# Row scatters of the first feed-forward block: the memset behind each one is left out

## The reference

```python
x = x + 0.5 * ffn(layernorm(x))
x = x + attn(layernorm(x))          # 16 heads of 8, causal, 2 x 1024 tokens
x = x + 0.5 * ffn(layernorm(x))

def ffn(x):                         # one shared and 7 routed experts, hidden width 352, top 2
    expert = lambda h, g, u, d: (silu(h @ g.T) * (h @ u.T)) @ d.T
    probs = softmax(x @ wr.T + rb)
    scores, idx = top_k(probs, 2);  scores = scores / scores.sum(-1)
    w = sum(scores * one_hot(idx))
    return expert(x, sg, su, sd) + sum(w[e] * expert(x, rg[e], ru[e], rd[e]) for e in range(7))
```

## Time and profile before

| what | value |
|---|---|
| median of 3 runs | 571.84 us (570.95 to 572.29) |
| profiled execution, own time | 571.84 us |
| its span, first to last instruction | 570.0 us |
| PE / PEld busy | 521.1 us (91%) / 406.0 us (71%) |
| DVE / ACT busy | 388.5 us (68%) / 319.8 us (56%) |
| POOL busy | 272.1 us (48%) |
| mean granted PE clock | 0.972 |
| indirect DMAs of the sort in f = 0 (L1174) | 32, 34.4 us busy, 24.8 to 77.1 us |
| memsets at L1184 into the scratch tensor | 66 in both blocks, 0.43 us each |

### The profile page before, as it was taken

The page is one execution under the profiler, slowest core; times in us unless marked ns, Lnnn a source line. Parts: engine busy times, 40 slices in busy tenths (PEclk is TensorE's granted clock), DMA queues, the critical chain, the costliest instruction groups (busy, mean ns, idle before and its releaser), DMA issues.

```text
span 570.0 us, 11374 instructions
## 1 busy us (share of the span) xinstructions
PE 521.1 (91%) x3574; PEld 406.0 (71%) x3574; DVE 388.5 (68%) x1013; ACT 319.8 (56%) x678; POOL 272.1 (48%) x417
## 2 busy tenths in 40 slices
PE   5985969999996799999999999999999889889995
PEld 2884969998954465656666666565746889889995
DVE  5694635557367888887979888888555775445744
ACT  4552424457444276776767677677776444434643
POOL 8299887667356711212120303030318888854540
PEclk9899789999996899999999999999999999999999
DMA  8922424132861581505050505020001031431414
GB/s 283 294 67 50 111 77 120 45 107 81 242 183 56 170 190 35 173 2 175 2 174 1 176 0 176 1 102 2 2 2 33 31 91 43 118 92 34 125 50 121
DMA packets 41384, 54.65 MB, mean 96 GB/s; under 512 B 6064, under 2 KB 32176, under 8 KB 40560
## 3 DMA queue, kind: packets, MB, share of 16 engines
q1 hardware_dynamic: 32528, 42.70, 26.4%
q0 software_dynamic: 4480, 9.25, 4.9%
q10 hardware_dynamic: 4320, 1.98, 1.3%
HBM read 34.03 MB, written 28.00 MB: 109 GB/s over the span
## 4 chain that ended last, share of the span: by engine, by line
PE 57%; issue 18%; POOL 10%; DMA 6%; DVE 4%; SPq 2%; ACT 2%; ACTq 1%; another core or an unknown queue 1%; POOLq 0%; DVEq 0%
PE psum L1605 11%; PE psum L1648 11%; PE psum L1677 10%; PE psum L933 6%; POOL z_rows L1174 6%; PE psum L919 3%; PE psum L901 3%; PE psum L899 3%; PE psum L900 3%; PE psum L1608 2%; POOL idle L1184 2%; DMA b_p<-in_attn_c_proj_b 2%; DMA yc<-y_rows 1%; DMA y_rows<-ys,to_row 1%; PE psum L1633 1%
## 5 line engine op out<-in xcount | busy, mean ns | idle before, releaser
L1757 DVE TENSOR_REDUCE mxp<-psum 128x1 f32<-128x512 f32 (+3 forms) x304 | 179.0, 654 | 32.9 <-PE psum L1605 32.1
L1816 ACT ACTIVATE probs<-psum 128x512 f32<-128x512 f32 (+1 forms) x304 | 154.9, 578 | 39.8 <-PE psum L1648 37.2
L1863 POOL TENSOR_SCALAR_AFFINE_SELECT probs<-probs 128x512 f32<-128x512 f32 x64 | 40.0, 635 | 174.2 <-ACT probs L1816 174.2
L1648 PE MATMUL psum<-queries,keys 128*128 128x512 f32 (+3 forms) x384 | 122.5, 381 | 0.6 <-DMA queries<-m_rows 0.3
L1605 PE MATMUL psum<-keys,queries 128*128 128x512 f32 (+1 forms) x304 | 116.1, 417 | 2.9 <-DVE mxp L1757 2.4
L1000 ACT ACTIVATE silu<-psum 128x352 f32<-128x352 f32 x107 | 49.6, 463 | 99.5 <-PE psum L901 62.6
L1197 POOL DMA_INDIRECT y_rows<-ys,to_row x76 | 74.3, 977 | 59.1 <-DVE ys L1079 35.4
L1043 DVE TENSOR_TENSOR act<-silu,psum 128x352 f32<-128x352 f32 x107 | 55.6, 519 | 68.0 <-ACT silu L1000 41.7
L933 PE MATMUL psum<-wall_f,at 128*128 (+1 forms) x648 | 92.2, 279 | 2.7 <-DVE x L1081 1.8
L1648 PEld LDWEIGHTS psum<-queries,keys 128*128 128x128 f32 x384 | 66.8, 191 | 26.8 <-ACT probs L1816 12.6
L933 PEld LDWEIGHTS psum<-wall_f,at 128*128 128x128 f32 x648 | 82.1, 194 | 4.1 <-ACT at L1008 2.3
(11 more groups left out here) (240 smaller groups left out, 732.4 us busy)
## 6 DMA issues: line engine op xcount, KB each, us to landing
z_rows<-q_stack SPq DMA_DIRECT2D x12, 682.5 KB, 5.6
keys<-k_stack SPq DMA_DIRECT2D x32, 128.0 KB, 5.9
queries<-q_stack SPq DMA_DIRECT2D x8, 512.0 KB, 5.3
zg_early<-z_rows SPq DMA_DIRECT2D x44, 65.0 KB
yc<-y_rows SPq DMA_DIRECT2D x10, 256.0 KB, 4.0
zg_late<-z_rows SPq DMA_DIRECT2D x32, 65.0 KB
k_stack<-zt_h SPq DMA_DIRECT2D x8, 256.0 KB, 2.9
q_stack<-q_h SPq DMA_DIRECT2D x8, 256.0 KB, 3.7
```

The costliest lines, as they stand in the source:

```text
L1648: ins = e.matmul(slot(K, u, d, n)[:, m * (q1 - q0):(m + 1) * (q1 - q0)], K.keys[v][:, j, kt * P:(kt + 1) * P], K.queries[v][:, q0:q1], sta ...
L1757: e.tensor_reduce(K.mxp[:, heads[0]:heads[-1] + 1, i, which], scores, AX.X, ALU.max).then_inc(K.A["taken"], 1)
L1816: e.activation(probs_of(K, product)[:, heads[0]:heads[-1] + 1, :], src, ACT.Exp, scale=SCALE).then_inc(K.A["ex"], 1)
```

## The change

In sort_pool the memset behind the indirect DMA is now written only for f = 1. In f = 0 the 30 memsets behind the DMAs of tiles 1 to 7 (14, part 0) and 8 to 15 (16, part 1) are gone. The indirect DMAs, their order, their data and their semaphores are the same, as are the memsets of f = 1 and those behind the first ten scatters of y_rows in both blocks.

```diff
     e.indirect_dma_start(K.z_dram[f], bass.IndirectOffsetOnAxis(ap=K.slots[:, g:g + 1], axis=0),
                          K.zrow[f][:, t, :], None).then_inc(K.z_sc[t // HALF], 16)
-    if g % TT > 0:
+    if f == 1 and g % TT > 0:
         pause_pool(K, f == 1 and t < HALF)
```

## The result

The changed kernel takes 578.38 us (median of 4 runs, 577.09 to 579.91) and the kernel before, on the same chip, 571.76 us (4 runs, 570.95 to 572.29). The medians differ by 6.6 us. The ratio is worked out from all 35 recorded runs of the changed kernel (575.98 to 582.40 us, mean 579.37): 1.0134, with a 95% interval of 1.0101 to 1.0168. It is slower. Two executions of the kernel before on the chips of the later experiments were in a slower state (578.63 and 730.11 us), and the ratios leave them out. The prediction was 560.8 us, with a range that ended at 566.8. It was wrong in sign. The profiled execution after took 579.51 us with a span of 577.7 (571.84 and 570.0 before); its granted clock was 0.968 (0.972).

A forecast was written before the change was run, and what follows sets the result against it. PE bounds the kernel, with two waits set by the end of POOL's scatters. 8.65 us gained at step 21 plus 2.4 us of clock, 11.05 in all, take 571.84 to 560.8 us; range 558.6 to 566.8.

The forecast's parts named there:

- Pitch: POOL's scatters in f = 0: start to start 1.26 us instead of 1.56, 0.30 us gained per removed memset.
- rival C: Scatter pitch stays 1.56 us without memsets, limited by DMA engines or POOL's descriptor making; time 571.8 us; chance 0.07.
- The 16th: Last scatter of the first half of the f = 0 sort: to end at 48.3 us instead of 52.10, 3.8 us earlier.
- DVE: Small DVE instructions held by denser scatters: each 0.55 us better or worse at most, 2.7 us on PE's path; nothing taken.
- The first wait of PE: PE before the first sorted transposes: there at 51.53, starts at 52.6 instead of 56.44, wait 1.1 us instead of 4.9.
- a sign of being wrong: PE's first sorted tiles (step 13): the prediction is wrong if PE comes to them later than 52.5 us.
- 1.2 us to spare: Places for the 17th scatter: written until 47.39, ahead of its possible start at 48.6, so not the later wait.
- The clock: PE's granted clock held through shortened waits: 2.65 us less after the first wait, 2.4 us more behind the second.
- Part 1: Second 16 scatters of f = 0: 4.8 us shorter, 32nd ends at 68.5; step 21 at 73.4 instead of 82.05.
- The time behind it: From 88 us on: PE at 9 tenths, everything behind released by it, so the gain stays; f = 1 shifted, not shortened.
- Rival D: DVE, needing the memset gaps, held until 48.3 and 18 us late, PE's shared tiles with it; 580 us; chance 0.06.

The follow-up runs named there:

- part 0 alone: Kernel before with only the 14 memsets of the first 16 scatters in f = 0 left out, the other 16 kept: 572.81 us, ratio 0.9993.

## Why the prediction was wrong

**Pitch (right).** It was 1.26 us in all of f = 0 without DVE's long subtractions, so rival C (1.56 stays) falls. The 16th ended 2.4 us earlier than forecast. The first scatter began 1.4 us earlier in that execution (23.37 instead of 24.77), and only three scatters met a long subtraction instead of four: DVE, late itself by then, started the fourth at 48.22 instead of 43.40, behind the 16th scatter. The working had kept DVE's subtractions in their places.

**DVE (right, as far as it went).** No instruction of DVE waited for the end of a run of scatters: L784 takes 0.17 us and L1482 1.25 in the middle of one. DVE's timeline of the changed kernel:
```profile
27.16 1.25 DVE L1482 TENSOR_TENSOR wall<-nat_g,wall 128x1056 fp32r<-128x1056 f32 x1
28.53 0.17 DVE L784 TENSOR_SCALAR d_cnt<-d_cnt 128x8 f32<-128x8 f32 x1
...
51.66 0.17 DVE L750 CAST slots<-d_slot 128x16 int32<-128x16 f32 x1
```
The rule of the Trainium skill (SBUF — State Buffer, "Who interferes with whom") was weighed as the one that speaks against the change. By it, an instruction of DVE loses at most one scatter; the largest lateness here is several scatters long and is measured on ACT as well as on DVE, so it isn't that rule at work.

**The first wait of PE (the step that failed).** The prediction said "PE is there at 51.53, since the tiles of the shared expert don't depend on the scatters". By data they don't. But each of their steps goes from PE to ACT to DVE and back, and with the scatters at 1.26 us each hand-over from PE came up to 5.0 us late. PE was there at 56.03 instead of 51.53, and it began the sorted tiles at 55.88, past the 52.5 that the prediction named as a sign of being wrong. With it the places of part 1 came at 51.84, 4.45 us late. The 1.2 us to spare that the prediction had worked out for them went with the rest, and the 17th scatter started at 52.65 instead of 48.6.

**The clock (followed from it).** The forecast held it at full speed, because waits were to be short. PE waited 7.38 and 5.15 us instead, and the mean from 53 to 73 us was 0.74 (0.83 before). It also fell ahead of the first wait: from 45.79 to 49.20 us it was at the lower level of 1.2 GHz, where it was at full speed before.

**Part 1 (its first half right).** 32nd scatter forecast for 68.5, seen at 72.54, all of which is the late start; its 16 pitches are 1.26 us. But step 21, forecast at 73.4, came at 91.01. It no longer waits for the sort at all: PE's down product L933 is right ahead of it, without an idle gap. PE was late by its own steps, held up to 8.2 us each in part 1, and the list rows_at came at 86.82 instead of 73.02 for the same reason.

**The time behind it (right).** Whatever step 21 is early or late by stays in good part to the end: it was late by 8.96 us and the span is 7.7 longer; the last scatter of y_rows in f = 0 starts at 165.58 instead of 158.96, 6.6 us late, which is also the difference of the medians.

**Rival D (right number, wrong cause).** It gave 580 us, slower, "the memsets are what lets DVE in", and PE's shared tiles late with DVE. The loss has this form and nearly this size, but what the gap lets in is PE's increments, and it had a chance of 0.06. The argument that lowered it (L853 and L750 end with the scatter they meet) was about one engine. There was no row in the profile before that showed a run of scatters at 1.26 us with PE's hand-overs beside it, only two scatters in a row. The gap was priced at what it costs, 0.30 us, and not at what it may be there for; its range below nothing was left out.

**What stays open.** Which resource fills is not shown: all that the traces show is that increments of PE and issues of SP are late together while POOL issues indirect DMAs densely. PE's ends are modelled by the profile, so it isn't shown either whether PE's last write or its increment is what waits. Every execution on record was also recorded for its spans, so whether the recording itself is a part of the load is untested. Nor is it shown how much of the difference between the parts is more than their pitch, why part 1 is later still when part 0 was kept in pace (11.2 us against 8.2), and why six scatters of y_rows in f = 0 don't do it. That the time of part 0 alone is equal to before, with up to 4.9 us of lateness, I would put down to PE waiting 4.90 us there anyway; that is argued, not tried.

## What to carry to other kernels

A delay between DMA issues that looks like idle filler may be what the other engines' hand-overs live on; before it is removed, ask what else runs in the stretch, and try half of it. When PE, ACT and DVE are all idle at once, compare the end of each producer with the start of its consumer: a wait that has no busy engine in front of it is a late signal. And a pace can be tuned by itself: memsets of 256 and 320 columns instead of 384, pitches of 1.45 and 1.51 us instead of 1.56 between ordinary scatters, gave 4.2 us here, and 1.26 cost 6.6.

## What the runs showed of the hardware

- Indirect DMAs of 128 rows of 520 bytes take POOL 0.96 us each and can follow at 1.26 us. In a run of 16 at that pitch PE's semaphore increments reach ACT and DVE up to 5.0, 8.2, 11.2 and (in f = 1) 14.2 us after PE's instruction has ended; at 1.56 us mostly 0.0 to 0.1, at most 1.3 in the sort of f = 0 and 1.7 in f = 1 of the kernel before, with scatters of y_rows and loads of SP at once. Increments of ACT and DVE in the same stretch were on time (0.04 and 0.14 us).
- It depends on the mean pitch over some scatters: gaps of 0.30, 0.30 and 1.07 us (mean pitch 1.52) gave 2.1 us, even gaps at 1.51 gave 2.4 and 3.5, and the largest lateness in part 1 was 6.9 us at 1.46 and 9.6 at 1.40.
- Four indirect DMAs that met a DVE subtraction of 1056 or 1408 columns with both inputs in SBUF took 1.52 to 2.38 us in the kernel before, and three took 1.69 to 1.80 in the changed one.
- SP's issuing is slowed as well: seven issues in 5.80 us instead of 3.48, and in 8.48 us with memsets of one column.
